# Two kinds of one-hots written by VectorE in another element order, in a graph-attention layer on one Trainium2 core

## The reference

```
q = (X @ Wq)[src];  k = (X @ Wk)[dst]           # 64 features each
e = tanh(q + k)
scores = e @ Wphi;  exp_scores = exp(scores - max(scores))
alpha = exp_scores / (segment_sum(exp_scores, src)[src] + 1e-9)
msg = alpha[:, None] * ((X @ Wy_w + Wy_b)[dst] + e @ We)
out = layernorm(X + segment_sum(msg, src))
```

## Time and profile before

| what | value |
|---|---|
| median of 3 runs | 5694.43 us (5687.73 to 5695.09) |
| the profiled execution | 5686.2 us, of which its span (first to last instruction) is 5684.4 us |
| mean granted TensorE clock | 0.746 |
| main part | about 4180 us of the span |
| sort part | about 1010 us |

### The profile page before, as it was taken

The page is one execution under the profiler, slowest core; times in us unless marked ns, Lnnn a source line. Parts: engine busy times, 40 slices in busy tenths (PEclk is TensorE's granted clock), DMA queues, the critical chain, the costliest instruction groups (busy, mean ns, idle before and its releaser), DMA issues. The chain is left out here.

```text
span 5684.4 us, 96987 instructions
## 1 busy us (share of the span) xinstructions
PE 4185.9 (74%) x26293; PEld 3173.4 (56%) x26293; DVE 3813.0 (67%) x8693; ACT 2687.2 (47%) x8743; POOL 3462.9 (61%) x3560
## 2 busy tenths in 40 slices
PE   7899999996667667667666766666676666666667
PEld 6744444444555555555555555555555555555556
DVE  6599999997655555655555555566555555555556
ACT  3467777775343444433344334434443344433346
POOL 1012222223777777777777777777777777777771
PEclk9956666656777777777787777777777777777778
DMA  2200000001333333333333333333333333333334
GB/s 84 70 3 4 4 4 4 4 4 39 100 107 105 105 105 105 105 105 105 105 105 105 105 105 105 105 105 107 107 105 105 105 105 105 105 105 105 105 97 107
DMA packets 279582, 478.44 MB, mean 84 GB/s; under 512 B 91964, under 2 KB 198878, under 8 KB 278814
## 3 DMA queue, kind: packets, MB, share of 16 engines
q0 software_dynamic: 166144, 326.27, 21.5%
q1 hardware_dynamic: 95132, 140.96, 7.8%
q10 hardware_dynamic: 17794, 4.91, 0.4%
HBM read 456.42 MB, written 20.60 MB: 84 GB/s over the span
## 5 line engine op out<-in xcount | busy, mean ns | idle before, releaser
L987 POOL DMA_INDIRECT gathered<-table,dst_rows x3296 | 3147.1, 955 | 1034.7 <-issue 965.1
L1022 PE MATMUL bank<-gathered,weighted_onehots 128*128 128x193 f32 x6592 | 1804.5, 434 | 363.4 <-DVE block_sums L1094 350.0
L1011 PE MATMUL bank<-q_parts,src_onehots_T 128*128 x9888 | 1136.4, 217 | 965.7 <-DVE src_onehots_T L1056 717.7
L1022 PEld LDWEIGHTS bank<-gathered,weighted_onehots 128*128 128x128 f32 x6592 | 1507.4, 257 | 421.0 <-ACT weighted_onehots L1042 347.7
L1011 PEld LDWEIGHTS bank<-q_parts,src_onehots_T 128*128 128x128 bf16 x9888 | 869.8, 106 | 1391.7 <-issue 1189.2
L1094 DVE TENSOR_TENSOR block_sums<-block_sums,bank 128x193 f32 x3296 | 1166.0, 354 | 528.4 <-issue 193.5
L1031 ACT ACTIVATE gathered<-gathered 128x256 f32<-128x256 f32 x824 | 346.2, 420 | 2180.7 <-DVE gathered L1070 2180.7
L1070 DVE TENSOR_TENSOR gathered<-bank,gathered 128x256 f32<-128x256 f32 x824 | 349.3, 424 | 1118.7 <-DMA gathered<-table,dst_rows 1099.5
L1042 ACT ACTIVATE weighted_onehots<-src_onehots,edge_weight 128x128 f32<-128x128 bf16 x3296 | 1073.4, 396 | 26.9
L770 ACT ACTIVATE col_records<-col_onehots,record_low 128x64 f16<-128x64 bf16 x3223 | 803.6, 424 | 262.2 <-DVE col_onehots L718 262.2
L811 POOL DMA_INDIRECT sorted_list<-sorted_groups,unit_destinations x248 | 294.8, 1189 | 885.1 <-DVE sorted_groups L747 823.1
(11 more groups left out here) (176 smaller groups left out, 2026.4 us busy)
## 6 DMA issues: line engine op xcount, KB each, us to landing
src_in_block_rows<-src_in_block_list SPq DMA_DIRECT2D x206, 512.0 KB, 3.8
gathered<-table,dst_rows POOLq DMA_INDIRECT x3296
table<-in_x SPq DMA_DIRECT2D x4, 1562.5 KB
x_in<-in_x SPq DMA_DIRECT2D x24, 256.0 KB, 2.8
x_again<-in_x SPq DMA_DIRECT2D x48, 128.0 KB, 2.3
out<-out_rows SPq DMA_DIRECT2D x48, 128.0 KB, 1.9
sorted_list<-sorted_groups,unit_destinations POOLq DMA_INDIRECT x248, 2.3
table<-k_and_q ACTq DMA_DIRECT2D x24, 128.0 KB, 2.0
```

The source lines that it names most:

```text
L987: e.indirect_dma_start(slot[:, r, j, 0:ROW], None, table, bass.IndirectOffsetOnAxis(ap=gidx[:, t:t + 1].bitcast(u32), axis=0)).then_inc(ga ...
L1011: made = e.matmul(QK[q % 2][:, j * A:(j + 1) * A], ohT[:, c % 2, o:o + PARTS], q3[:, bass.ds(b + s_ * A, A)], start=s_ == 0, stop=s_ == 2)
L1022: made = e.matmul(SM[q % 2 * 2 + j // 2][:, o:o + SUMS], ohw[:, q % 3, j, :], slot[:, r, j, A:SLOT], start=True, stop=True)
```

## The change

Line 1056 keeps its one instruction and its 2048 elements, but goes over them in two halves, the even elements first and then the odd ones, so that neighbours in the order of work lie 4 bytes apart, in the input and in the output. Line 1059, one instruction over 4 x 128 x 4 elements with the tile innermost, becomes four instructions of 4 x 128 elements, one for each quad of the chunk, with the place innermost: neighbours in the output and in `row1c` lie 8 bytes apart, and `lo` is repeated over the innermost dimension. What is in memory afterwards is the same in both cases, and so are the semaphores; the fourth of the new instructions signals.

```diff
+        def spread_inner(col, n, m):
+            return col.rearrange("p (n a) -> p n a", a=1).to_broadcast([PARTS, n, m])
...
-                    e.tensor_scalar(ohT[:, c % 2, :], lob[:, c % LOB, :], part0[:, :], None, ALU.is_equal).then_inc(onehots_T_made, 1)
+                    e.tensor_scalar(ohT[:, c % 2, :].rearrange("p (n h) -> p h n", h=2), lob[:, c % LOB, :].rearrange("p (n h) -> p h n", h=2),
+                                    part0[:, :], None, ALU.is_equal).then_inc(onehots_T_made, 1)
                     if c >= 2:
                         e.wait_ge(weighted, (c - 1) * QUADS_PER_CHUNK)
-                    e.tensor_tensor(oh[:, c % 2, :, :, :], lo[:, c * CHUNK:(c + 1) * CHUNK].rearrange("p (q a j) -> p q a j", a=1, j=QUAD)
-                                    .to_broadcast([PARTS, QUADS_PER_CHUNK, PARTS, QUAD]),
-                                    row1c[:, :, :].rearrange("p (a n) j -> p a n j", a=1).to_broadcast([PARTS, QUADS_PER_CHUNK, PARTS, QUAD]),
-                                    ALU.is_equal).then_inc(onehots_made, 1)
+                    for i in range(QUADS_PER_CHUNK):
+                        made = e.tensor_tensor(oh[:, c % 2, i, :, :].rearrange("p a j -> p j a"),
+                                               spread_inner(lo[:, c * CHUNK + i * QUAD:c * CHUNK + (i + 1) * QUAD], QUAD, PARTS),
+                                               row1c[:, :, :].rearrange("p a j -> p j a"), ALU.is_equal)
+                    made.then_inc(onehots_made, 1)
```

## The result

| | before | after |
|---|---|---|
| median | 5693.54 us (4 runs, 5687.73 to 5695.09) | 6012.6 us (4 runs, 6003.86 to 6017.6) |
| ratio, with its 95% interval | | 1.056 [1.0543, 1.0577] |
| the profiled execution | 5686.2 us | 6012.46 us, span 6010.7 us |
| mean granted TensorE clock | 0.746 | 0.709 |

A forecast was written before the change was run, and what follows sets the result against it. GpSimd's gap-free gather queue was taken as the bound; gather holds from lines 1056 and 1059, 1.22 us per chunk in place of 0.157, add 219 us to 5686.2, giving 5905, stated as 5900; 8-in-10 range 5800 to 6120.

The forecast's parts named there:

- The bound: Main part: 3296 GpSimd gathers queue without a gap, 0.955 us plus a 0.30 us pause each, 4136 of 4162 us.
- Line 1056: Its two halves take 1.28 us, 1.39 with waits, instead of 0.75; the chunk's first gather gets an excess of 0.65 us.
- Line 1059: One element per tick: four pieces of 0.68 us, starting 0.60 apart, 2.48 together, instead of 1.2 us.
- The upper bound of 1.11 us: Longest expected piece of line 1059, at 0.84 per element over 1.04 ns, taken from line 1226's reads stepping 772 bytes.
- The evidence against slow steps: ScalarE's lines 1042 and 770 with 8-byte steps took 0.89 ns per element, the same as adjacent ones in line 910.
- pair rule: Skill: VectorE's full rate only for adjacent 4-byte pairs, 1.98 ns when three streams hop; pieces of line 1059 about 1.16 us.
- The moment of asking: 0.14 us after its start a gather needs what VectorE holds, waits for that instruction's end and ends 0.82 us later.
- a hold of 0.56: The chunk's second gather asks at 3013.62 and waits for the third piece until 3014.16: excess 0.56 us.
- the first rival: Steps of 8 bytes are slow: pieces of 1.11 us, two gathers held 0.80 us each, +431 us, 6120; chance 21%.
- Beside the path: VectorE's extra 1.6 us per chunk fits its 5.3 us of waiting; TensorE's sums have over 4 us to spare: no cost.
- Line 1056 at one element per tick: Rival: line 1056 takes 2.35 us and no longer holds GpSimd: +30 us, 5725, or 5855 with slow pieces; chance 11%.
- That only packed work holds GpSimd: Rival: with no two elements adjacent neither line holds gathers, the 0.157 us excess goes: -32 us, 5662; chance 7%.

The follow-up runs named there:

- adjacent_but_unpacked: The changed kernel with the output of old line 1059 stored tile by tile and its constants adjacent, `lo` still repeated: 5809.46 us, 1.0208 against the kernel before.
- constants_step_only: The changed kernel with the output stored tile by tile, so only the constants are read with 8-byte steps: 6394.88 us, 1.0052 against before (6359.39 us).
- changed_again: The changed kernel, unedited, run again on the first kind of chip: 6010.53 us, 1.0564 against the kernel before (5691.93 us).
- one_instruction: The changed kernel with its four pieces made by one instruction in the same order of elements: 7068.57 us, 1.1028 against the kernel before (6409.64 us).
- output_step_only: The changed kernel with adjacent constants, so only the pieces' output has 8-byte steps: 6479.42 us, 1.0175 against the kernel before (6359.39 us).
- constants_in_psum_2: The changed kernel with the pieces' constants read as fp32 from PSUM, leaving one input in SBUF: 5879.64 us, 1.0335 against the kernel before (5691.93 us).

## Why the prediction was right in kind and 113 us short

The forecast was 5900, the time is 6012.6, inside the range. By its steps:

**The bound.** Right. The gathers' queue without a gap sets the time: +325.6 us of busy time, +326.3 of span, pauses of 0.30 as before.

**Line 1056.** Right. Forecast 1.28 us, 1.39 with its waits; the shortest is 1.35, so (1.35 - 0.216) / 1024 = 1.11 ns for two elements, and the mean 1.474 in the group above. The first gather's excess is 0.67, forecast 0.65. It is the one large disturbance left in *adjacent_but_unpacked*. The same place of the chunk has 0.11 of the 0.157 before, so 206 x (0.67 - 0.11) = 115 of that kernel's 118 us are its share.

**Line 1059.** Mis-sized: 0.68 us forecast, 1.32 measured. Four pieces in 4.69 us are (4.69 - 0.15) / 2048 = 2.22 ns for each element, where 1.04 was taken from adjacent operands. The upper bound of 1.11 us was too low as well: it came from line 1226, which reads with a large step and writes adjacent elements, and reading with steps of 8 bytes is free (*constants_step_only*). The evidence against slow steps came from ScalarE, another engine. VectorE's writes with a step had no row at all, and the bound should have been set wider for that.

The Trainium skill's pair rule ("Vector Engine (DVE) Microarchitecture Reference", Measured stream behaviour on trn2), weighed there and not taken, had the right direction and three quarters of the size: an estimate of 1.16 us by its 1.98 ns for three hopping streams, 0.48 of the 0.64 missing. The table of that section of the Trainium skill, for 4-byte words, also has rows that the prediction did not use: 1.73 ns with one source hopping, 1.71 with the destination hopping, and 2.50 to 2.51 with both sources, or the destination alone, stepping by 24 words. The 2.22 measured here lies between. On the two sides the Trainium skill and the measurement differ, and the measurement decides: here the input's step costs nothing and the output's 1.18 ns for each element.

**The moment of asking.** Failed for instructions with two inputs, and it hid behind the size. "0.14 us after its start a gather needs something that VectorE holds" is wrong by 0.18 us for them. Counted over the main parts of all fourteen traces, an instruction with two inputs in SBUF that starts 0.25 to 0.05 us before a gather's recorded start holds it in all 2163 cases, and at 0.04 us before in all 12. One that starts from 0.03 before to 0.30 after holds none of 1706, where nothing else that holds is running at the gather's start. So what counts is which of these VectorE runs 0.04 us before the gather's recorded start. The trace of before had 13 such starts between 0.03 before and 0.13 after, all without a hold, as here:

```profile
2021.02 0.95 POOL L987 DMA_INDIRECT gathered<-table,dst_rows  x1 [0.30 <-issue]
2021.02 0.45 DVE L1078 TENSOR_TENSOR e_times_phi<-gathered,phi 128x256 f32<-128x256 f32 x1
```

One edge is open. Where a gather starts within 0.03 us of such an instruction that follows directly on another of VectorE's holders, it is held by the second in 17 cases of 1435: 12 of 194 third gathers in the changed kernel, most of the 0.08 above, and none of 192 in *changed_again*.

The line of the transposed one-hots follows another rule, and neither the prediction nor this moment covers it. In halves (1.35 us) and started 0 to 0.46 us *after* a gather's recorded start it holds the gather in all 662 cases, until it ends, and the gather ends 0.12 to 0.13 later: 3016.42 + 1.35 + 0.12 = 3017.89 in the chunk of *adjacent_but_unpacked* above, and 3030.05 in *one_instruction* likewise. From 0.47 on the gather is free and the line waits instead. On the first kind of chip this is rare (8 gathers and 5.9 us of the changed kernel, against 197 and 135 us where the line starts first); in *one_instruction* and *output_step_only* it is the usual case, 117 and 118 us.

With the right moment, the forecast's own pieces of 0.68 hold nothing: the gather of 3013.48 meets the second piece (3012.88 to 3013.56), which ends before it would matter, and not the third, which starts at 3013.48. That gives 0.65 - 0.157 = 0.49 us per chunk, 5787 us for the profiled execution. *adjacent_but_unpacked* bears it out (5808.65 us, second gather 0.02); of the 22 us between, some 10 are the 0.05 us of excess elsewhere in a chunk, which was there before and which this sum drops. It is a narrow escape: in 192 of its 206 chunks a piece starts 0.00 to 0.01 us after the second gather, and 0.05 us earlier it would have held it. So two wrong steps partly cancelled: too short pieces, and a hold of 0.56 that pieces of that length don't cause. That the time came out inside the range is partly luck.

**What happened in place of it.** A released gather ends 0.82 us after the release, and the next starts 0.30 later, 1.12 us after it in all. The pieces start as far apart; by the trace's single records those of the chunk shown start at 3007.23, 3008.31, 3009.45 and 3010.59. The gather of 3008.43 finds the second piece 0.12 us old and waits it out: it ends at 3010.28, 0.82 after 3009.46, which is 0.19 before the reported end of the piece (3009.65). The next starts at 3010.58, when the fourth piece has not yet begun, and is free. So the first rival was nearest: right in kind on the pieces (slow by their steps, though 1.32 and not 1.11) and on its first meeting (0.80 forecast, 0.88 measured), and wrong in the second (0.80 forecast, 0.08 measured): 5905 forecast, 6120 the rival, 6012 measured.

**Beside the path.** Right. VectorE's longer work was hidden: its wait fell by 462 us and was not used up, and GpSimd never waited for the ring. *constants_in_psum_2* shows where the cover has a hole: a later line 1078 (now 1083) meets other gathers.

**The other rivals.** Line 1056 at one element per tick: no, 1.35 us. That only packed work holds GpSimd: refuted by both holds, and by the 4.79 us of *one_instruction*. That nothing changes: no.

Open are the cost of the pieces alone on the first kind of chip, why VectorE gets gathered rows later on the second, why a gather and line 1056 meet in two ways, and why a hold by a writing with steps ends 0.2 us before VectorE's reported end (also 3036.05 against 3031.88 + 4.79 - 0.82 = 3035.85 in *one_instruction*), where in the earlier trace rows the two agree within 0.02. The next instruction of VectorE starts at that same moment, at 3009.45 and at 3035.84.

## What to carry to other kernels

Where GpSimd issues indirect DMAs without a pause, look at each VectorE instruction not for its busy time but for what it holds up: here two inputs in SBUF hold, and so does line 1056 with its one input; two inputs of which one is in PSUM do not; and a hold ended with the one instruction that was met. An output of bf16 with a step of 8 bytes cost twice the time of an adjacent one, so put the step on the input side. When a meeting of two engines hangs on a tenth of a microsecond, count it over all the cases in the trace instead of reading it off one.

## What the hardware showed that was not expected

- Writing bf16 with a step of 8 bytes costs VectorE 2.22 ns for each element, against 1.04 adjacent; reading with that step costs nothing (0.691 us for a piece of 512, 0.687 adjacent).
- A gather is held by line 1056 even when that line starts up to 0.46 us after it (662 of 662 cases), but by an instruction with two inputs in SBUF only when that one starts at least 0.04 us before it.
- Four instructions take VectorE no longer than one (4.69 against 4.70 us), but they let GpSimd in between: 0.88 us of hold instead of 3.8.
- The same kernel took 5692, 6359 and 6410 us on three chips; on the slower two VectorE gets gathered rows later, and why is not shown. *output_step_only*, nearly the changed kernel (only its constants are adjacent), loses 1.8% on the second kind, where the changed kernel loses 5.6% on the first.
- TensorE's mean granted clock fell from 0.746 to 0.709 and cost nothing here: GpSimd's waits that end with TensorE went from 94 to 3 in 2000 us, none over 0.3 us. Why it fell is not shown; *adjacent_but_unpacked*, at 5809 us, kept 0.747.
